# A two-layer graph network: packing, joins and loads in another order, and the positive accumulators scaled by VectorE instead of ScalarE

## What is computed

```python
Wh = h @ W
e = (Wh @ a1)[:, None] + (Wh @ a2)[None, :]
e = where(e > 0, e, 0.2 * e);  e = where(adj > 0, e, -9e15)
x = layernorm(x + elu(softmax(e, axis=1) @ Wh))
x1 = adj @ x / adj.sum(1)
x = layernorm(x + concatenate([x1, x], 1) @ weight + bias)
```

## Time and profile before

| what | value |
| --- | --- |
| median of 3 runs | 1609.38 us (1608.64 to 1609.53) |
| the profiled execution | 1609.33 us, its span 1607.4 us |
| PE busy, matmuls | 1495.1 us (93%), 13894 |
| DVE busy | 983.8 us (61%), 2786 instructions |
| ACT busy | 970.5 us (60%), 2384 instructions |
| POOL busy | 116.9 us (7%) |
| mean granted TensorE clock | 0.977 of 2.4 GHz |
| chain that ended last, by engine | PE 33%, ACT 30%, DVE 24%, issue 9% |
| layer 0 / layer 1 on PE | from 59.5 us / from 1097.2 us |

### The profile page before, as it was taken

One profiled execution on the slowest core, in us unless ns is written; L12 is line 12 of the kernel. 1 busy time (PEld: TensorE's weight loads), 2 busy tenths in 40 slices (PEclk: granted clock), 3 DMA queues, 4 the chain that ended last, 5 costly groups with the idle time before them and its releaser, 6 DMA issues.

```text
span 1607.4 us, 38356 instructions
## 1 busy us (share of the span) xinstructions
PE 1495.1 (93%) x13894; PEld 1298.3 (81%) x13894; DVE 983.8 (61%) x2786; ACT 970.5 (60%) x2384; POOL 116.9 (7%) x199
## 2 busy tenths in 40 slices
PE   6487998999999899989999999998999999999998
PEld 6366787888888788878878888887888888888886
DVE  7986576677767767767777677664443444344343
ACT  3797789998988899899989888980100000010000
POOL 1001010001001000100010010000000000000000
PEclk9698999999999999999999999999999999999999
DMA  9957968867775787687677755013000000000000
GB/s 169 114 56 82 105 71 91 87 79 78 89 89 71 85 90 85 70 91 87 79 78 89 89 71 69 14 48 100 17 20 16 16 16 16 16 16 20 16 16 16
DMA packets 99714, 101.59 MB, mean 63 GB/s; under 512 B 4704, under 2 KB 66912, under 8 KB 99680
## 3 DMA queue, kind: packets, MB, share of 16 engines
q0 software_dynamic: 33792, 67.11, 42.0%
q1 hardware_dynamic: 65888, 34.03, 8.2%
HBM read 289.77 MB, written 12.68 MB: 188 GB/s over the span
## 4 chain that ended last, share of the span: by engine, by line
PE 33%; ACT 30%; DVE 24%; issue 9%; DMA 1%; ACTq 1%; DVEq 1%; SPq 0%; POOL 0%; POOLq 0%
PE acc L691 29%; ACT level_ring L424 27%; DVE edge_ring L895 5%; DVE level_ring L888 4%; DVE adj_space L839 2%; PE turn_ps L715 2%; PE acc L617 2%; DVE edge_ring L830 2%; ACT part_sums L435 1%; DVE adj_space L842 1%; DVE words L817 1%; DVE rows_y L987 1%; ACT words L403 1%; DVE row_sums L930 1%; DVE row_sums L938 1%
## 5 line engine op out<-in xcount | busy, mean ns | idle before, releaser
L424 ACT ACTIVATE level_ring<-s_row,cols 128x256 fp8e4<-128x256 f32 x2048 | 832.2, 498 | 0.0
L617 PE MATMUL acc<-factors,edge_ring 128*128 128x258 f16 x4096 | 558.0, 276 | 59.0 <-ACT part_sums L435 50.2
L617 PE MATMUL acc<-factors,level_ring 128*128 128x258 f16 x4096 | 558.2, 276 | 8.0 <-DVE row_sums L917 8.0
L691 PE MATMUL acc<-factors,adj_space 128*128 128x258 f16 x4096 | 469.4, 273 | 4.5 <-issue 4.5
L617 PEld LDWEIGHTS acc<-factors,edge_ring 128*128 128x128 fp8e4 x4096 | 367.5, 98 | 120.7 <-issue 64.6
L691 PEld LDWEIGHTS acc<-factors,adj_space 128*128 128x128 fp8e4 x4096 | 399.3, 97 | 63.6 <-issue 4.7
L617 PEld LDWEIGHTS acc<-factors,level_ring 128*128 128x128 fp8e4 x4096 | 367.8, 98 | 65.4 <-issue 8.3
L888 DVE TENSOR_TENSOR level_ring<-level_ring,edge_ring 128x1024 uint16<-128x1024 uint16 x256 | 174.2, 691 | 185.6 <-ACT level_ring L424 174.7
L581 PE MATMUL pack_ps<-pack_w,adj_space 128*128 128x32 bf16 x1024 | 172.4, 177 | 23.3 <-DVE adj_space L842 23.3
L522 ACT ACTIVATE part_sums<-acc 128x258 f32<-128x258 f32 x32 | 12.4, 386 | 297.4 <-PE acc L691 297.4
L895 DVE TENSOR_TENSOR edge_ring<-edge_ring,level_ring 128x1024 uint16<-128x1024 uint16 x256 | 166.7, 684 | 0.0
(11 more groups left out here) (92 smaller groups left out, 729.8 us busy)
## 6 DMA issues: line engine op xcount, KB each, us to landing
adj_space<-in_adj POOLq DMA_DIRECT2D x64, 1024.0 KB, 15.5
x_parts<-parts SPq DMA_DIRECT2D x32, 129.0 KB, 2.9
factors<-x_parts SPq DMA_DIRECT2D x8, 516.0 KB, 6.8
factors<-in_x SPq DMA_DIRECT2D x8, 512.0 KB, 7.2
s_row<-s_and_t SPq DMA_DIRECT2D x32, 128.0 KB, 2.9
rows_x<-in_x SPq DMA_DIRECT2D x32, 128.0 KB, 3.0
x_rows<-rows_y SPq DMA_DIRECT2D x32, 128.0 KB, 9.8
rows_x<-x_rows SPq DMA_DIRECT2D x32, 128.0 KB, 2.1
```

The lines of the kernel that those rows point to most:

```text
L424: a = act.activation(level_bytes[:, h % MASK_SLOTS, j, :], s_row[:, slot, :], ACT.Relu, bias=t_big[:, h * HALF + j:h * HALF + j + 1], scal ...
L617: m = pe.matmul(acc[a][:, 0:ROW], mask, factors[:, neg, jj, :], start=(jj == 0), stop=(jj == NJ - 1))
L691: m = pe.matmul(acc[b][:, 0:ROW], ring_1_bytes[:, c, j, b * P:(b + 1) * P], factors[:, 0, jj, :], start=(jj == 0), stop=(jj == NJ - 1))
```

## The change

It has five parts.

- ACT's `copy_positive` is gone. In `add_negative` DVE scales each positive accumulator itself (a `tensor_scalar` from PSUM to `part_sums`), in the order copy 0, add 1, copy 2, add 3.
- ACT's `high_parts` moves from after block 1 to after block 4.
- On SP, `load_x` goes ahead of `store_x1`.
- The first round isn't joined: PE packs each of its chunks straight from the bytes, with four matmuls a tile, accumulated, and weights for each of the four row tiles (`pack_bits`).
- Rounds 1 and 2 are joined, packed and copied in other places, group by group (the dictionaries of `group` on DVE, PE and ACT). From group 4 on the places are those of before.

```diff
@@ -89,7 +89,7 @@
         consts_sb = sb("consts_sb", [P, P + WPT], F32)
-        pack_w = sb("pack_w", [P, WPR], BF16)
+        pack_w = sb("pack_w", [P, TILES, WPR], BF16)
         s_row = sb("s_row", [P, 2, GROUP], F32)
@@ -267,8 +267,8 @@
                 if not first:
+                    load_x(g)
                     store_x1(g - 1)
-                    load_x(g)
 
@@ -426,15 +426,6 @@
 
-            def copy_positive(g, first=False):
-
-                if not first:
-                    act.wait_ge(elu_ok, g)
-                for b in range(TPG):
-                    act.wait_ge(acc_done, 3 * g + 2 * b + 1)
-                    act.activation(part_sums[:, b, :], acc[2 * b][:, 0:ROW], ACT.Copy,
-                                   scale=u_col[:, bass.ds(TPG * g + b, 1)]).then_inc(pos_copied, 1)
-
             def exponential(g):
@@ -456,10 +447,8 @@
                         act.wait_ge(f_low_ok, UPG)
-                    if h == 1 and not second:
+                    if h == UPG and not second:
                         high_parts(g - 2, before_last)
-                    if h == 2:
-                        copy_positive(g - 1, second)
                     if h % 2 and h // 2 in next_words:
@@ -484,16 +473,15 @@
                     act.activation(v_col, vy_col, ACT.Exp).then_inc(exp_cols_ok, 1)
-            group(1, 1, 1, {2: (1, 0), 3: (1, 1)}, second=True)
-            group(2, 0, 2, {0: (1, 2), 1: (1, 3), 3: (2, 0)}, before_last=True)
-            group(3, 1, 2, {1: (2, 1), 3: (2, 2)})
+            group(1, 1, 1, {3: (1, 0)}, second=True)
+            group(2, 0, 2, {0: (1, 1), 1: (1, 2), 3: (1, 3)}, before_last=True)
+            group(3, 1, 2, {0: (2, 0), 1: (2, 1), 3: (2, 2)})
             with act.Fori(2, NR - 1) as n:
                 group(PAIR * n, 0, n + 1, {1: (n, 3), 3: (n + 1, 0)})
                 group(PAIR * n + 1, 1, n + 1, {1: (n + 1, 1), 3: (n + 1, 2)})
             group(NG - 2, 0, NR, {1: (NR - 1, 3)})
             group(NG - 1, 1, NR, {})
             high_parts(NG - 2)
-            copy_positive(NG - 1)
             exponential(NG - 1)
@@ -570,20 +558,25 @@
 
-            def packable(n, c, first=False):
-                pe.wait_ge(joined_ok, UPG * n + c + 1)
-                if not first:
-                    pe.wait_ge(words_ok, UPG * n + c - 1)
+            def packable(n, c):
+                pe.wait_ge(joined_ok, UPG * (n - 1) + c + 1)
+                pe.wait_ge(words_ok, UPG * n + c - 1)
 
             def pack_tile(c, j):
 
                 nibbles = adj_ring[:, c, 0, j * P:(j + 1) * P].bitcast(F8)
-                return pe.matmul(pack_ps[c % 2][:, j * WPR:(j + 1) * WPR], nibbles, pack_w[:, :], start=True, stop=True)
-
-            def pack(c):
-
+                return pe.matmul(pack_ps[c % 2][:, j * WPR:(j + 1) * WPR], nibbles, pack_w[:, 0, :], start=True, stop=True)
+
+            def pack_bits(c):
+
+                pe.wait_ge(adj_in[c], 16)
+                if c >= 2:
+                    pe.wait_ge(words_ok, c - 1)
                 for j in range(UNIT):
-                    m = pack_tile(c, j)
+                    for t in range(TILES):
+                        bits = adj_ring[:, c, t, j * P:(j + 1) * P].bitcast(F8)
+                        m = pe.matmul(pack_ps[c % 2][:, j * WPR:(j + 1) * WPR], bits, pack_w[:, t, :],
+                                      start=(t == 0), stop=(t == TILES - 1))
                 m.then_inc(packed, 1)
@@ -595,9 +588,8 @@
             pe.matmul(turn_ps[1][:, 0:F], sum_xb, wq[:, 0:F], start=True, stop=True).then_inc(mean_made, 1)
-            pe.wait_ge(pack_w_ok, TILES)
-            packable(0, 0, first=True)
-            pack(0)
+            pe.wait_ge(pack_w_ok, 2 * TILES - 1)
+            pack_bits(0)
 
@@ -636,16 +628,17 @@
                 if c < UPG - 1:
-                    packable(0, c + 1, first=(c == 0))
-                    pack(c + 1)
+                    pack_bits(c + 1)
                 for h in (2 * c, 2 * c + 1):
                     multiply(0, h, h % 2 == 0, True)
-            group(1, 1, {c: c for c in range(UPG)})
-            with pe.Fori(1, NR - 1) as n:
-                group(PAIR * n, n + 1, {1: 0, 3: 1})
-                group(PAIR * n + 1, n + 1, {1: 2, 3: 3})
-            group(NG - 2, NR, {})
-            group(NG - 1, NR, {})
+            group(1, {1: (1, 0), 2: (1, 1), 3: (1, 2)})
+            group(2, {1: (1, 3), 2: (2, 0), 3: (2, 1)})
+            group(3, {1: (2, 2), 3: (2, 3)})
+            with pe.Fori(2, NR - 1) as n:
+                group(PAIR * n, {1: (n + 1, 0), 3: (n + 1, 1)})
+                group(PAIR * n + 1, {1: (n + 1, 2), 3: (n + 1, 3)})
+            group(NG - 2, {})
+            group(NG - 1, {})
 
@@ -746,10 +739,13 @@
                     dve.wait_ge(pack_w_ok, i)
-                    dve.scalar_tensor_tensor(out=pack_w[:, :], in0=digit, scalar=weight, in1=pack_w[:, :],
+                    dve.scalar_tensor_tensor(out=pack_w[:, 0, :], in0=digit, scalar=weight, in1=pack_w[:, 0, :],
                                              op0=ALU.mult, op1=ALU.add).then_inc(pack_w_ok, 1)
                 else:
-                    dve.tensor_scalar(pack_w[:, :], digit, weight, None, ALU.mult).then_inc(pack_w_ok, 1)
+                    dve.tensor_scalar(pack_w[:, 0, :], digit, weight, None, ALU.mult).then_inc(pack_w_ok, 1)
+            dve.wait_ge(pack_w_ok, TILES)
+            for t in range(1, TILES):
+                dve.tensor_scalar(pack_w[:, t, :], pack_w[:, 0, :], 2.0 ** t, None, ALU.mult).then_inc(pack_w_ok, 1)
 
@@ -838,14 +834,13 @@
                                          op0=ALU.logical_shift_left, op1=ALU.bitwise_or).then_inc(joined_tiles, 1)
-                dve.wait_ge(joined_tiles, UPG * n + c + 1)
+                dve.wait_ge(joined_tiles, UPG * (n - 1) + c + 1)
                 dve.scalar_tensor_tensor(out=joined[:, c, 0, :], in0=joined[:, c, TPG, :], scalar=TPG,
                                          in1=joined[:, c, 0, :], op0=ALU.logical_shift_left, op1=ALU.bitwise_or)\
                     .then_inc(joined_ok, 1)
 
             make_product(0)
             make_product(1)
-            join(0, 0)
             dve.tensor_scalar(y_col, s_col, t_max, None, ALU.add).then_inc(y_ok_col, 1)
@@ -909,6 +904,9 @@
                 for b in range(TPG):
+                    dve.wait_ge(acc_done, 3 * g + 2 * b + 1)
+                    dve.tensor_scalar(part_sums[:, b, :], acc[2 * b][:, 0:ROW], u_col[:, bass.ds(TPG * g + b, 1)], None,
+                                      ALU.mult).then_inc(pos_copied, 1)
                     dve.wait_ge(pos_copied, TPG * g + b + 1)
@@ -993,19 +991,19 @@
                     normalise(g - 2, rstd_ok, x1_ok)
-                for c in joins.get(0, ()):
-                    join(n + 1, c)
+                if 0 in joins:
+                    join(*joins[0])
                 masks(n, q, 1, "sums", second)
-                for c in joins.get(1, ()):
-                    join(n + 1, c)
+                if 1 in joins:
+                    join(*joins[1])
                 masks(n, q, 2, "softmax")
                 if not second:
                     low_parts(g - 2)
-                for c in joins.get(2, ()):
-                    join(n + 1, c)
+                if 2 in joins:
+                    join(*joins[2])
                 masks(n, q, 3)
-                for c in joins.get(3, ()):
-                    join(n + 1, c)
+                if 3 in joins:
+                    join(*joins[3])
                 elu_and_residual(g - 1, second)
@@ -1014,7 +1012,6 @@
                     make_product(2 * c + 3)
-                    join(0, c + 1)
                 masks(0, 0, c)
@@ -1022,10 +1019,12 @@
             dve.wait_ge(one_row_ok, 1)
-            group(0, 1, {c: (c,) for c in range(UPG)}, second=True)
-            with dve.Fori(1, NR - 1) as n:
-                group(n, 0, {0: (0,), 3: (1,)})
-                group(n, 1, {0: (2,), 3: (3,)})
+            group(0, 1, {0: (1, 0), 1: (1, 1), 2: (1, 2)}, second=True)
+            group(1, 0, {0: (1, 3), 2: (2, 0), 3: (2, 1)})
+            group(1, 1, {0: (2, 2), 3: (2, 3)})
+            with dve.Fori(2, NR - 1) as n:
+                group(n, 0, {0: (n + 1, 0), 3: (n + 1, 1)})
+                group(n, 1, {0: (n + 1, 2), 3: (n + 1, 3)})
             group(NR - 1, 0, {})
```

More of the change, by code:

```diff
@@ L626, in multiply, with group @@
                     w.then_inc(packed, 1)
-            def group(g, n, packs):
+            def group(g, packs):
                 for c in range(UPG):
                     for h in (2 * c, 2 * c + 1):
-                        pack_chunk = packs.get(c) if h % 2 else None
+                        n, pack_chunk = packs.get(c, (0, None)) if h % 2 else (0, None)
                         if pack_chunk is not None:
```

## The result

| | before | after |
| --- | --- | --- |
| median of 4 runs | 1609.01 us (1608.12 to 1609.53) | 1531.46 us (1529.64 to 1533.03) |
| span of the profiled execution | 1607.4 us | 1530.4 us |

The ratio is 0.9518, with a 95% interval of 0.9502 to 0.9535: 4.8% less. The forecast was 1529.6.

A forecast was written before the change was run, and what follows sets the result against it. No engine was full; ACT, waiting for DVE before the high parts, set layer 0's period of 31.5 us against PE's 29.36. 1609.3 - 58.7 (steady stretch) - 21.0 (start) = 1529.6 us, range 1521 to 1553.

The forecast's parts named there:

- step 5: Start of layer 0: with four joins gone from DVE, group 1 starts at about 103.4, not 106.19: 2.8 us won.
- step 6: Stalls of 11.2 and 8.6 us before group 4 go; with step 5, 21 us saved by group 4's start.
- (4): Steady stretch of layer 0 from group 4: 29.36 us a group instead of 31.5, 58.7 us saved.
- Step 1: ACT's loop in layer 0: without 0.7 of copies and 3.4 of waiting, 27.4 us a group, below PE's 29.36.
- Step 2: DVE's two added copies a group: 0.45 us each, 0.9 a group, 29 us in all, covered by DVE's idle time.
- Step 3: Group boundaries in layer 0: DVE reaches the first copy in time for PE, with 1.6 us to spare.
- A: Rival, layer 0's hand-overs: a remainder of the wait stays, groups take 30.2 us, total 1552; chance 0.20.
- B: Rival, layer 0: only the start is won, ACT's wait returns at the exponential, total 1569 us; chance 0.07.
- C: Rival, group boundaries: DVE becomes the bound and the kernel slower, 1625 us at 3 us a copy; chance 0.03.
- D: Rival, the start: third adj load stalls group 3 by 3 to 6 us, 1533 to 1536; within the main forecast's 0.68.

The follow-up runs named there:

- experiment 5: Changed kernel with SP's order of before, stores of x1 ahead of the next load of x: 1536.55 us.
- experiment 3: Kernel before with one edit, ACT's high parts moved from after block 1 to after block 4: 1545.53 us.
- experiment 7: Changed kernel with the first round joined by DVE again and packed with 16 small multiplies a chunk: 1533.61 us.
- Experiment 1: Changed kernel with ACT's high parts back after block 1, the copies staying on DVE: 1569.99 us.
- experiment 2: Changed kernel with the positive accumulators' copies back on ACT, the high parts staying after block 4: 1530.83 us.
- experiment 4: Kernel before with the high parts moved after block 4 and the copies on DVE, on the old start: 1550.02 us.
- experiments 8 and 9: Changed kernel with three, then nine dummy additions on DVE ahead of each group's first copy: 1531.45 and 1586.32 us.
- experiment 6: Changed kernel with joins, packings and word copies of rounds 1 and 2 back in their old places, first round still packed from bytes: 1542.9 us.

## Why the prediction was right

**The sum.** Forecast and profile, in us:

| step | forecast | measured |
| --- | --- | --- |
| start of group 1 (step 5) | 103.4 | 103.66 |
| start of group 2 (5) | 133.1 | 133.42 |
| start of group 3 (6) | 162.8 | 163.18 |
| start of group 4 (6) | 192.2 | 192.56 |
| length of a group (4) | 29.36 | 29.38 |
| end of layer 0 | 1013.0 | 1013.8 |
| PE stands between the layers | 4.5, as before | 5.25 |
| layer 1 | 510.2, as before | 511.4 |

The end of layer 0 is 1092.67 - 79.7 in the forecast and 956.59 + 57.20 in the profile. The profiled span passes its forecast (1607.4 - 79.7 = 1527.7) by 2.7 us: 0.8 to the end of layer 0, 0.75 between the layers and about 1.1 in layer 1. The prediction took the last two as before. They vary from trace to trace where no edit touches them: the pause from 4.0 to 5.3 us, layer 1's first 160 matmuls from 19.4 to 20.9. One doesn't explain the other. Here are experiment 5, with a pause of 5.2 ahead of them, and experiment 3, with one of 4.5:

```profile
1023.82 19.40 PE acc L684 x160
```

```profile
1033.06 20.84 PE acc L691 x160
```

So no cause is shown for these 1.9 us. The start of group 1 varies too, by 2.8 us between traces (experiment 7): that it came within 0.3 of the forecast, and the later starts with it, is partly luck. The lengths of the groups behind it don't vary so.

**Step 1 was the change.** Experiment 1 priced it by the prediction's own numbers, 1570 forecast and 1569.99 measured: ACT at 27.4 + 3.4 us a group (30.7 measured) is above PE, without the 3.4 below it. Experiment 3 shows it alone, 63.5 us. The reading that found it was that of two waits, 109.4 and 50.2, the one that PE shows is the smaller and the later: PE waits for ACT's copy because ACT is late, and ACT is late because of a wait that PE has no part in.

**Step 2, the copies,** cost 0.485 us each (0.45 taken) and nothing in time; experiment 2 shows that leaving them out changes nothing once the high parts have moved. I had named the gain in step 1 together with them ("ACT's copies go"), and of its two terms, 0.7 and 3.4, the 0.7 wasn't needed: ACT at 28.1 is still under PE. The Trainium skill (Advanced Engine Details and Errata, TRN2 Errata) says that ScalarE is the one closer to PSUM. The traces agree on the direction: ACT's copy has a median of 0.472 us in experiment 2, DVE's 0.485 in the changed kernel. The difference is too small to decide where a copy goes here. What decides is which engine is late: in the old start it is DVE, and there the copies on DVE cost 4.3 us (experiments 3 and 4); with the high parts in their old place it is ACT, and there taking the copies off it is worth about 20, by the estimate in experiment 1.

**Step 3, DVE's room,** was forecast as 1.6 us and is 2.4 (experiments 8 and 9). DVE's join ended at 512.70 (512.01 + 0.69), 26.2 us after the end of the group before (515.9 - 29.38 = 486.5), where I had 27.1. 0.4 of this is a slip in the sum: the 16.1 counts from DVE's hand-over, at E + 10.6, and I added it to the exponential's start, at E + 11. The other 0.5 is that the two groups of a round differ: the one read in the earlier trace rows takes 16.1, its like in the changed kernel 16.0 (its join ends at E + 26.6), the one here 15.6. The mechanism was right, the size on the safe side.

**Steps 5 and 6** held in their sum, 20.7 us against 21, and the parts, undone one by one, give 2.2 (first round, forecast 2.8), 11.4 (joins) and 5.1 (SP's order). These add up to 18.7, and with all three undone at once, in experiment 4, the time is 18.6 above the changed kernel's, so each gives its part whether the others are there or not. The rest of the 21 is not the start's. Step 1 wins 6 us before group 4 (experiment 3), which the prediction booked under the stalls, and the copies on DVE would have lost 4.3 of them in the old start. That the two nearly cancel is luck.

**The rivals.** A (a remainder of the wait) would have shown as PE's waits for the copies; it has 1.9 us. B fell with the 0.27 before the exponential, unchanged; its sum, 1569, is what experiment 1 measures (1569.99) with the wait left in its old place. C, DVE as the bound, is real beyond 2.4 us of room: nine dummy additions bring 1586 us. To lose all of the 77.6 us over 29 boundaries it would have needed 2.7 us of lateness beyond that room at each, 5.1 in all (2.4 + 2.7); the copies are of 0.485 us. D: the third join started at 159.91 without a wait.

## What to carry to other kernels

Where no engine is full, list every wait of the engine that the fullest one waits for, and ask of each whether the thing waited for needs the waiter's own next output: a finished group's copy placed just behind the block that its producer must treat first stops both once a group. Moving such an instruction three blocks later cost nothing here and was worth 63.5 us, more than all offloading. Before moving work between engines, work out each engine's loop without its waits; if the crowded one is then under the bound, remove the wait first and leave the work where it is. The order of trying matters: by the estimate in experiment 1 the copies alone would have looked like a gain of about 20 us, and they are worth nothing once the high parts have moved. At a start, look for what stands in program order behind a DMA that hasn't landed, such as a copy behind a join, or a load behind a store that waits.

## What was not expected of the hardware

Reading a flag from SBUF into a register of PE and branching on it left PE idle for 4.0 to 5.3 us between the layers; with the reading two groups earlier 1.9 and 2.4 stayed. And a stop can be dearer than its length: after 7.8 us of waiting in experiment 6 PE's granted clock was at its lower level, 1.2 GHz, and blocks of eight took 1.88 us instead of 1.05 before it returned to 2.4, which cost 2.7 us more. Shorter stops did so in some places only. In the kernel before twelve groups start behind the same pause of 2.3 us, and at six of them the clock fell:

```profile
276.40:278.00 1.60, 1.60 (x15) 1.40 (x16) 1.49 (x6) 1.60 (x5) 0.00 (x0) 1.00 1.05 119
339.50:341.00 1.50, 1.46 (x8) 1.08 (x9) 1.34 (x5) 1.50 (x5) 0.00 (x0) 0.55 1.06 120
```

There it cost no time, since ACT set the pace: group 8, which starts at 339.55 with the clock at 0.55, is as long as group 6, which starts at 276.39 at 1.00 (31.3 us). No run here shows what makes the difference.
